# Attention outputs multiplied in place in two buffers, stores in order of arrival, first operands loaded during the projection

## What is computed

```python
h = _layernorm(x) * (1 + ca) + sa
c_kv = h @ W_kv_down
k_rope = _rotary_apply(c_kv @ W_k_rope, cos, sin)
k = (c_kv @ W_k_up).reshape(Bb, Tt, NH, HD)
v = (c_kv @ W_v_up).reshape(Bb, Tt, NH, HD)
q = (h @ W_q).reshape(Bb, Tt, NH, HD)
q_rope = _rotary_apply(h @ W_q_rope, cos, sin)
scores = einsum('bqhd,bkhd->bhqk', q, k) + einsum('bqr,bkr->bqk', q_rope, k_rope)[:, None]
w = softmax(where(causal, -inf, scores / sqrt(HD + D_R)))
x = x + ga * (einsum('bhqk,bkhd->bqhd', w, v).reshape(Bb, Tt, D_MODEL) @ W_o)
h = _layernorm(x) * (1 + cb) + sb
x = x + gb * ffn(h)
```

## Time and profile before

| | |
|---|---|
| three timed executions | 4112.24, 4124.86 (median) and 4128.85 us |
| the profiled execution | 4117.91 us, span 4116.2 us |
| PE busy | 3737.5 us, 91% of the span |
| DVE, POOL, ACT busy | 69%, 59%, 43% |
| granted clock of PE, mean | 0.952 of full speed |
| projection's last matmul ends | 472.3 us |
| attention's first matmul | 501.46 us |
| attention's last output multiplied | 3238.80 us |

### The profile page before, as it was taken

The page is one execution under the profiler, slowest core; times in us unless marked ns, Lnnn a source line. Parts: engine busy times, 40 slices in busy tenths (PEclk is TensorE's granted clock), DMA queues, the critical chain, the costliest instruction groups (busy, mean ns, idle before and its releaser), DMA issues. The chain is left out here.

```text
span 4116.2 us, 57078 instructions
## 1 busy us (share of the span) xinstructions
PE 3737.5 (91%) x19808; PEld 2428.7 (59%) x19808; DVE 2840.8 (69%) x5454; ACT 1789.5 (43%) x3401; POOL 2436.3 (59%) x1145
## 2 busy tenths in 40 slices
PE   7999679889898899989999899889999699999998
PEld 4777445555555555555555555555555377777777
DVE  5777477767667677776777767767667277777776
ACT  2333235445454454544545445454455233333332
POOL 1333237666675676766766668666676555555555
PEclk9999889999999999999999999999999799999999
DMA  5888863462534534435345353362531211111110
GB/s 181 286 290 285 252 126 75 87 129 64 109 77 95 120 75 98 102 71 121 74 96 115 74 120 75 80 136 61 112 75 45 105 51 61 61 61 61 61 61 31
DMA packets 238409, 438.40 MB, mean 107 GB/s; under 512 B 25332, under 2 KB 26868, under 8 KB 238072
## 3 DMA queue, kind: packets, MB, share of 16 engines
q1 hardware_dynamic: 238136, 435.68, 41.2%
q10 hardware_dynamic: 64, 0.02, 0.0%
HBM read 300.86 MB, written 134.23 MB: 106 GB/s over the span
## 5 line engine op out<-in xcount | busy, mean ns | idle before, releaser
L800 ACT ACTIVATE att_probs<-att_ps_s 128x512 f32<-128x512 f32 (+3 forms) x2560 | 1304.0, 533 | 1414.7 <-PE att_ps_s L955 1306.8
L906 POOL TENSOR_TENSOR att_sum_g<-att_sum_g,att_probs 128x2048 f32<-128x2048 f32 (+3 forms) x384 | 1442.5, 3757 | 195.0 <-ACT att_probs L800 159.7
L836 DVE TENSOR_REDUCE att_piece_max<-att_ps_m 128x1 f32<-128x512 f32 x1536 | 994.2, 683 | 236.9 <-PE att_ps_m L940 230.7
L954 PE MATMUL att_ps_s<-att_q_a,att_k_a 128*128 128x512 f32 (+3 forms) x2560 | 963.3, 380 | 26.5 <-DMA att_q_b<-att_neg_max 24.7
L955 PE MATMUL att_ps_s<-att_q_b,att_k_b 65*128 65x512 f32 (+3 forms) x2560 | 939.3, 371 | 0.0
L940 PE MATMUL att_ps_m<-att_k_a,att_q_a 128*128 128x512 f32 (+3 forms) x1840 | 680.0, 395 | 183.6 <-DVE att_piece_max L839 130.7
L839 DVE CUSTOM_DVE_ANT_0 att_ps_m<-att_ps_m,mask_qk 128x128 f32<-128x128 f32 (+3 forms) x1024 | 490.5, 508 | 322.9 <-PE att_ps_m L940 314.8
L940 PEld LDWEIGHTS att_ps_m<-att_k_a,att_q_a 128*128 128x128 f32 x1840 | 346.3, 195 | 545.7 <-DVE att_piece_max L839 250.9
L961 PE MATMUL att_ps_o<-att_probs,att_v 128*32 128x512 f32 (+3 forms) x5120 | 620.2, 557 | 5.1 <-POOL att_probs L884 5.1
L954 PEld LDWEIGHTS att_ps_s<-att_q_a,att_k_a 128*128 128x128 f32 x2560 | 492.9, 193 | 160.8 <-issue 74.4
L955 PEld LDWEIGHTS att_ps_s<-att_q_b,att_k_b 65*128 65x128 f32 x2560 | 491.0, 192 | 68.5
(11 more groups left out here) (173 smaller groups left out, 5197.6 us busy)
## 6 DMA issues: line engine op xcount, KB each, us to landing
att_q_a<-s_q_hi SPq DMA_DIRECT2D x128, 256.0 KB, 6.5
att_q_a<-s_qr_hi SPq DMA_DIRECT2D x128, 256.0 KB, 7.3
prj_x_sb<-in_x_dram SPq DMA_DIRECT2D x16, 1024.0 KB, 5.3
s_q_hi<-prj_q_hi SPq DMA_DIRECT2D x16, 1024.0 KB, 4.4
s_q_lo<-prj_q_lo SPq DMA_DIRECT2D x16, 1024.0 KB, 6.4
s_k_hi<-prj_k_hi SPq DMA_DIRECT2D x16, 1024.0 KB, 6.7
s_k_lo<-prj_k_lo SPq DMA_DIRECT2D x16, 1024.0 KB, 7.6
s_v<-prj_v_sb SPq DMA_DIRECT2D x16, 1024.0 KB, 8.8
```

The lines of the kernel that those rows point to most:

```text
L800: act.activation(probs[t % RING][:, hh, c0:CH], ps_s[(GH * t + hh) % SBANKS][:, c0:CH], ACT.Exp, scale=SCALE).then_inc(probs_ready, 1)
L836: dve.tensor_reduce(top, ps_m[:, bank, :], AX_X, ALU.max).then_inc(piece_taken, 1)
L906: pool.tensor_tensor(sum_g[:, :, c0:CH], sum_g[:, :, c0:CH], new, ALU.add).then_inc(sum_added, 1)
L954: mm(out[:, c0:CH], k_a[:, hh, i * P:(i + 1) * P], q_a[j][:, hh, c0:CH], start=True, stop=False)
```

## The change

- There are two buffers `o_sb0` and `o_sb1`, used in turn, and no `o_raw`. ACT copies `ps_o` straight into one of them and waits for the store two outputs before; DVE multiplies in place and no longer waits for a store.
- SP's list for a unit is in another order: the store of the last output of the unit before comes first, ahead of `k_next` and the next queries, and the other stores stand before `place_max` of the chunk two further on.
- The buffers of the keys `k_a`, the values `v`, `q_a` of chunks 0 and 1 and `q_b` of chunk 0 are allocated before the projection. SP loads unit 0's data into them after the stores of projection chunks 6 to 13, one group in each. Room for this comes from two buffers of the projection that now lie on raw weights no longer needed (`xn`, `rot_a`). SP's loop over the chunks is unrolled.
- The rotary parts are stored once per chunk, 64 KiB per store, and all head groups load the same copy.
- At the start of attention SP loads `k_b` of chunks 0 and 1 and `q_b` of chunk 1, waits until the first maximum has been placed, and then loads the rest.

```diff
-        xn = sb("xn", [P, TB, D], F32)
+        xn, up_raw = prj["weights"][2][0], prj["weights"][4][0]
...
-                    sp.dma_start(to_r[0][j][n], as_f32(rot[0][:, j, None, :]).broadcast_to([DR, NG, CH])).then_inc(st_r, 16)
+                    sp.dma_start(to_r[0][j][n], as_f32(rot[0][:, j, :])).then_inc(st_r, 16)
...
+            early = [lambda: load_k_a(0, 0), lambda: load_q_a(0, 0), lambda: load_k_a(0, 1), lambda: load_q_a(0, 1),
+                     lambda: load_k_a(0, 2), lambda: load_k_a(0, 3), lambda: [load_v(0, j) for j in range(TCH)],
+                     lambda: load_q_b(0, 0)]
+            for n in range(NCH):
+                body(n, n < NCH - 2, n < NCH - 1)
+                if FIRST_EARLY <= n < FIRST_EARLY + len(early):
+                    early[n - FIRST_EARLY]()
...
             def store_o(u, j):
                 wait_alone(sp, o_ready, TCH * u + j + 2, sp_mark)
-                sp.dma_start(scratch["o"][TCH * u + j], o_sb[:]).then_inc(o_stored, 16)
+                sp.dma_start(scratch["o"][TCH * u + j], o_sb[j % 2][:]).then_inc(o_stored, 16)
 
             def body(u, nxt):
+                if u:
+                    store_o(u - 1, TCH - 1)
                 if nxt:
                     load_k_next(u + 1)
                     wait_alone(sp, scores_ready, GH * (NSTEP * u + STEPS[0]), sp_mark)
                     load_q(u + 1, 0)
-                if u:
-                    store_o(u - 1, TCH - 1)
-                for j in range(1, TCH - 1):
-                    place_max(u, j + 1)
-                    store_o(u, j - 1)
-                    if nxt:
-                        wait_alone(sp, scores_ready, GH * (NSTEP * u + FIRST[j] + STEPS[j]), sp_mark)
-                        load_q(u + 1, j)
-                store_o(u, TCH - 2)
+                store_o(u, 0)
+                place_max(u, 2)
+                if nxt:
+                    wait_alone(sp, scores_ready, GH * (NSTEP * u + FIRST[1] + STEPS[1]), sp_mark)
+                    load_q(u + 1, 1)
+                store_o(u, 1)
+                place_max(u, 3)
...
-            for j in range(TCH):
-                load_k_a(0, j)
+            load_k_b(0, 0)
+            load_k_b(0, 1)
+            load_q_b(0, 1)
+            wait_alone(sp, m_in[0], 16, sp_mark)
+            for j in range(2, TCH):
                 load_q(0, j)
                 load_k_b(0, j)
-                load_v(0, j)
...
             def take_output(u, j):
                 act.wait_ge(pv_done, NSTEP * u + FIRST[j] + STEPS[j] + RING)
-                act.wait_ge(o_ready, TCH * u + j + 1)
-                act.copy(o_raw[:], ps_o[:]).then_inc(o_copied, 1)
+                if TCH * u + j >= 2:
+                    act.wait_ge(o_stored, 16 * (TCH * u + j - 1))
+                act.copy(o_sb[j % 2][:], ps_o[:]).then_inc(o_copied, 1)
...
             def normalise(u, j):
-                waits(dve, (rden_ready, TB * (TCH * u + j + 2)), (o_copied, TCH * u + j + 2), (o_stored, 16 * (TCH * u + j) + 1))
-                dve.tensor_tensor(o_sb[:], o_raw[:], rden[:], ALU.mult).then_inc(o_ready, 1)
+                waits(dve, (rden_ready, TB * (TCH * u + j + 2)), (o_copied, TCH * u + j + 2))
+                dve.tensor_tensor(o_sb[j % 2][:], o_sb[j % 2][:], rden[:], ALU.mult).then_inc(o_ready, 1)
```

More of the change, by code:

```diff
@@ L209, in projection_buffers, with projection @@
     return prj
-def projection(nc, keep, dram, scratch, prj):
+def projection(nc, keep, dram, scratch, prj, ops):
     with ExitStack() as ctx:
@@ L603, in attention @@
         sem = lambda n: ctx.enter_context(nc.semaphore("att_" + n))
-        k_a = sb("k_a", [P, GH, T], F32R)
+        k_a, v = ops["k_a"], ops["v"]
         k_b = sb("k_b", [2 * HD + 1, GH, T], F32R)
-        q_a = [sb(f"q_a{j}", [P, GH, CH], F32R) for j in range(TCH)]
-        q_b = [sb(f"q_b{j}", [2 * HD + 1, GH, CH], F32R) for j in range(TCH)]
-        v = sb("v", [P, TCH, TB, P], F32)
+        ops["q_a"] += [sb(f"q_a{j}", [P, GH, CH], F32R) for j in range(2, TCH)]
+        ops["q_b"] += [sb(f"q_b{j}", [2 * HD + 1, GH, CH], F32R) for j in range(1, TCH)]
+        q_a, q_b = ops["q_a"], ops["q_b"]
         probs = [sb(f"probs{i}", [P, GH, CH], F32) for i in range(RING)]
@@ L616, in attention @@
         neg_max = sb("neg_max", [GH * TB, TCH, P], F32R)
-        o_raw, rden, o_sb = (sb(n, [P, CH], F32) for n in ("o_raw", "rden", "o_sb"))
+        rden, *o_sb = (sb(n, [P, CH], F32) for n in ("rden", "o_sb0", "o_sb1"))
         ps_s = [ctx.enter_context(nc.psum_tensor(f"att_ps_s{i}", [P, CH], F32)) for i in range(SBANKS)]
@@ L1465, in adaln_block @@
         }
-        with ExitStack() as first:
-            prj = projection_buffers(nc, first)
-            setup(nc, keep, dram, scratch, prj)
-            projection(nc, keep, dram, scratch, prj)
-        attention(nc, keep, scratch)
+        with ExitStack() as held:
+            ops = operands(nc, held)
+            with ExitStack() as first:
+                prj = projection_buffers(nc, first)
+                setup(nc, keep, dram, scratch, prj)
+                projection(nc, keep, dram, scratch, prj, ops)
+            attention(nc, keep, scratch, ops)
         feedforward(nc, keep, dram, scratch, out)
```

84 lines of the change are left out of this document (48 added, 36 removed).

## The result

| | before | changed |
|---|---|---|
| median of the timed executions (4 each) | 4123.64 us | 3976.38 us |
| lowest to highest | 4112.24 to 4128.85 | 3967.03 to 3982.20 |
| profiled execution, its span | 4117.91, 4116.2 us | 3976.48, 3974.8 us |
| PE busy, share of the span | 3737.5 us, 91% | 3721.2 us, 94% |
| granted clock of PE, mean | 0.952 | 0.971 |

The ratio is 0.9644 (95% interval 0.9617 to 0.9672): 147 us less. The sum behind the forecast of 3961 us was 160 us less; the range, 3938 to 3995, holds the time.

What follows compares the result with a forecast made beforehand. PE was busiest, but stalled by DVE's waits for a late store and by the start of attention. Gains of 138.7 and 21.5 us, 160.2 together, gave 3957.7 or 3964.7, so 3961 us was forecast, range 3938 to 3995.

Steps and rivals of the forecast that it cites:

- The sum behind the forecast: Whole kernel: 138.7 us from the outputs and 21.5 us from the start of attention, 160.2 us less.
- the gain of these stretches: First outputs of units 1 to 14: each stretch falls to unit 15's 48.67 us, 138.7 us less in all.

Runs made afterwards that it cites:

- two numbers in the order: A unit's first output multiplication two steps later, the others one: 3878.70 us on the changed kernel, 3990.54 us on the kernel before.

## What to carry to other kernels

When one stage of a loop runs without a stall that the others have, subtract its window: that gave the gain of these stretches within a microsecond in one profile and 4.5 us in another, stall, clock and successor included. Look also for what lies outside the window; here 8 us came back there. Then look at what the freed engine meets next: here a 0.69 us instruction took up to 4.84 us by its place against another engine's additions, and two numbers in the order were worth 98 us on top of the change and 130 without it. Of a wait with two cures (another buffer, an earlier store) try each alone, since either may do, and read how much room each leaves: 2.1 us with the earlier store alone, 13.4 with the second buffer alone, 25.2 with both.

## What the hardware showed that I had not expected

- A multiplication of 128x512 f32 in SBUF on DVE takes 0.68 us alone and up to 4.84 when it starts just after the begin of a POOL addition of 4.6 us; the 512-column maxima, which read PSUM, take at most 0.69 us inside the same additions as outside them (747 and 789 of them in the changed kernel).
- How often a gap on PE brought the granted clock down (to 0.5, which is 1.2 GHz), in units 1 to 14: gaps of 1.1 us in no unit of any profile, of 1.27 us in 0 to 5, of 1.8 us in 4 to 13, and of 3.3 us or more in every unit that had one. So the same gap of 1.8 us did it in some units and not in others.
- The placing of the maxima, an 8 KB DMA issued by ACT, cost PE a wait of 6.5 to 8.8 us with SP's 256 KB loads under way and of 2.3 to 2.6 us without them.
